# Loading the next stage's weights and first rows inside the stage in front of it, in a transformer kernel of eleven stages

## The chip, the cores and the metric

The kernel runs on one core of a Trainium2 chip. The metric is device time in microseconds (us) of one execution; lower is better. The core has five engines that each work through their own list of instructions: TensorE (PE; PEld is its weight load), VectorE (DVE), ScalarE (ACT), GpSimd (POOL) and SyncE (SP), which here mostly starts DMA transfers. Engines wait for one another, and for transfers, by semaphores.

## What is computed

Eight layers follow one another on x (32 sequences of 256 rows of 256 numbers), with a context of 32 x 120 x 192:

```python
x = x + _L0_xattn_ref(_layernorm(x, axis=-1), ctx_768, ...)    # 16 heads, Wq Wk Wv Wo
x = x + _L0_ffn_ref(_layernorm(x, axis=-1), L0_ffn_w1, L0_ffn_conv_w, L0_ffn_conv_b, L0_ffn_w2)
x = x + _L1_xattn_ref(_layernorm(x, axis=-1), ctx_768, ...)
x = x + _L1_ffn_ref(_layernorm(x, axis=-1), ...)               # 8 experts, top 2
x = x + _L2_xattn_ref(_layernorm(x, axis=-1), ctx_768, ...)    # 16 heads
x = x + _L2_ffn_ref(_layernorm(x, axis=-1), ...)               # 4 gated experts
x = x + _L3_xattn_ref(_layernorm(x, axis=-1), ctx_768, ...)    # sparse attention, FiLM, S4D, MLP
x = x + _L3_ffn_ref(_layernorm(x, axis=-1), ...)               # low rank
```

The three parts that the change touches:

```python
def weight_quant(w):                                   # L0 ffn: ternary weights
    scale = 1.0 / jnp.clip(jnp.mean(jnp.abs(w)), 1e-05)
    return jnp.clip(jnp.round(w * scale), -1, 1) / scale
...
hid = jax.nn.relu(jnp.einsum('td,edh->teh', xf, ew1) + eb1[None, :, :])   # L2 ffn: gated experts
y = jnp.einsum('teh,ehd->ted', hid, ew2) + eb2[None, :, :]
out = jnp.einsum('te,ted->td', dense_w, y)
...
scale_out, shift_out = jnp.split(c_t @ W_film_out + b_film_out, 2, axis=-1)   # L3 xattn, second half
y = y * (1.0 + mod_gate * scale_out) + mod_gate * shift_out
xt = x_text + y
h = layernorm(xt, g_ffn, b_ffn)
h = jax.nn.gelu(h @ W1 + b1, approximate=False) @ W2 + b2
return layernorm(xt + h, g_norm_out, b_norm_out)
```

## The kernel before

A stage works through the 32 sequences, one tile of 256 rows (two blocks of 128) at a time, as a pipeline written out in full: `pipeline` goes over slots, and in each slot an engine does its step of one tile and later steps of earlier tiles. The stages, by the first letters of their tiles in the profile: `a` (heads_attention, `a0`), then, overlapping in one block, `f` (ternary_feed_forward, `f0`), `a1`, a router, `v` and the experts `e`; then `a` again (heads_attention, `a2`), `fa` (adaptive_with_sparse_attention: the gated experts and the first half of L3's attention), `cv` (convolve_channels, the state-space part as Toeplitz matmuls), `m` (modulated_feed_forward, `m3`) and, overlapping with it, `f` (low rank, `f3`).

Between `a0` and `f0`, `a2` and `fa`, `fa` and `cv`, and `cv` and `m3` there is a boundary: SP waits until the stores have landed, clears the stage's semaphores one by one (`end_all`), and all engines pass a barrier. Only then does the next stage's program begin. SP takes its list in order, and all plain transfers are started by it; the only others are GpSimd's indirect gathers in `a2` and the experts.

What each of the three stages does first, before:

- `f0` (`start` of its `sync` and `vector`, L843 and L908): SP requests w1 (1 MB) into the one buffer `wf`, then the convolution's taps and bias. DVE sums |w1| (L912), PE adds up over partitions (L1071), DVE makes mean and reciprocal (L914, L917) and in three passes the ternary w1 (L920 to L924). SP waits for the last pass (`w_all`), requests w2 into the same `wf`, and only behind that the first rows `xb` (L853); DVE does the same five steps with w2, and a sum over w2 (L927). `wmean` and `wscale` count on the semaphore `consts`, on which POOL's 24 products for `diag` (L882) count too, so the reciprocal waits for these.
- `fa` (L2311 to L2330): SP requests eight small weights, then rows `xb` of tiles 0 and 1, then the experts' w1 and w2 (2 MB each) and the rest. DVE, ACT and PE wait for the eight small ones (`small`), DVE then for `xb` (L209). Rows of tile 2 can be requested once tile 0 is normalised (`xn_ready`). Per tile the gate's matmuls (L2785, L2793, L2794) lead to softmax steps on DVE (L2512 on) and ACT (L2688, L2690), and then come the experts' matmuls (L2808, L2820).
- `m3` (L3029, L3031): SP requests twelve weights, 3.5 MB; all engines wait for all of them (`weights`, 192), then PE multiplies Wv and W_film_out into one matrix (L3210).

In `a0` a tile also sends its row minimum out (L387, `a_lowest`) and back to all partitions (L395, `a_floor`, two transfers of 960 KB), which DVE needs at L539. In `a2` POOL gathers four pieces of 128 KB per tile (L430), which DVE combines (L493). In `cv` each of 16 groups of channels needs 2 MB, `cv_toep` (L2908), into one of two buffers.

## Time and profile before

| | us |
|---|---|
| median of 3 runs | 4808.49 (4806.17 to 4809.97) |
| the profiled execution's own time | 4787.28 |
| its span | 4785.5 |
| PE busy | 4430.9, 93% |
| DVE busy | 3206.7, 67% |
| ACT / POOL busy | 2044.3 / 2082.9, 43% / 44% |
| mean DMA rate | 85 GB/s |

The profile is of one execution, and its rows carry times from the span's start. PE is busy nearly all the time inside the stages; in forty equal slices its busy tenths fall to 5 in two (around 600 to 700 us and 2000 to 2100 us) and to 6 or 7 in a few others. A row of a timeline names the start, the duration, the engine (SPq is SP's starting of a transfer), the line, what is written and read, and in brackets how long the engine had been idle and what ended that.

### The profile page before, as it was taken

The numbers are of one execution on the slowest core, as the hardware profiler recorded it, in microseconds if no ns is written. First come the engines' busy times: TensorE is split into PE (matmuls) and PEld (weight loads), VectorE is DVE, ScalarE is ACT, GpSimd is POOL, SyncE is SP. The second block draws the span as 40 slices with busy tenths as digits, with TensorE's granted clock in tenths as the row PEclk, the third lists the DMA queues.
The fourth block names the chain that finished last, engine by engine and source line by source line (L and its number), as shares of the span: only waits on it lengthen the run. The fifth ranks groups of instructions, "written<-read, shape, count | busy, mean of one in ns | idle before, by whom it ended". The sixth has DMA issues, their size and how long they took to land. (4 is left out here: it accounts for less than half of the span.)

```text
span 4785.5 us, 90713 instructions
## 1 busy us (share of the span) xinstructions
PE 4430.9 (93%) x31788; PEld 3449.3 (72%) x31788; DVE 3206.7 (67%) x9688; ACT 2044.3 (43%) x4216; POOL 2082.9 (44%) x2505
## 2 busy tenths in 40 slices
PE   7999859999999999959999799999999877999999
PEld 5666547778875888846666688888888744777866
DVE  6888779997553333147776399999999943444444
ACT  3555447764443332224444244444444332222244
POOL 2222136553454233044443365655656503565532
PEclk9999979999999999979999899999999988999999
DMA  4666512236333222122221211111111083232233
GB/s 115 154 154 155 131 56 74 75 109 183 67 87 104 82 71 71 49 77 71 69 69 36 84 35 34 42 33 35 41 34 38 22 266 103 90 96 85 92 111 102
DMA packets 333274, 407.33 MB, mean 85 GB/s; under 512 B 58932, under 2 KB 294165, under 8 KB 322070
## 3 DMA queue, kind: packets, MB, share of 16 engines
q1 hardware_dynamic: 315190, 368.41, 27.1%
q0 software_dynamic: 13312, 25.25, 2.2%
q10 hardware_dynamic: 4320, 7.87, 0.6%
q8 instruction: 256, 4.19, 0.4%
q14 instruction: 196, 1.61, 0.1%
HBM read 304.45 MB, written 96.96 MB: 84 GB/s over the span
## 5 line engine op out<-in xcount | busy, mean ns | idle before, releaser
L2808 PE MATMUL fa_h<-fa_xnT,fa_w 128*128 128x256 f32 x2048 | 474.9, 383 | 0.0
L2820 PE MATMUL fa_y<-fa_w,fa_hT 128*128 128x256 f32 x2048 | 462.5, 379 | 0.0
L2820 PEld LDWEIGHTS fa_y<-fa_w,fa_hT 128*128 128x128 f32 x2048 | 386.5, 190 | 65.3 <-issue 15.4
L2808 PEld LDWEIGHTS fa_h<-fa_xnT,fa_w 128*128 128x128 f32 x2048 | 380.6, 191 | 56.5 <-issue 9.4
L2701 ACT ACTIVATE fa_hT<-fa_h,fa_b 128x256 f32<-128x256 f32 x512 | 215.0, 470 | 476.8 <-PE fa_h L2808 411.4
L516 DVE TENSOR_REDUCE a_mx<-a_score 128x16 f32<-128x1920 f32 x128 | 275.9, 2156 | 78.5 <-PE a_score L700 68.7
L1945 POOL DMA_INDIRECT e_xg<-moe_rows,e_idx x64 | 128.7, 2011 | 322.2 <-issue 244.8
L3187 ACT ACTIVATE m_hT<-m_h,m_b 128x256 f32<-128x256 f32 x256 | 107.5, 471 | 364.7 <-PE m_h L3250 364.7
L1695 PE MATMUL r_h<-r_xnT,r_rw 128*128 128x256 f32 x1024 | 248.2, 391 | 5.7 <-ACT r_hT L1646 5.7
L219 POOL TENSOR_SCALAR a_rs<-a_mv 128x2 f32<-128x2 f32 x96 | 21.4, 223 | 531.0 <-DVE a_mv L213 527.4
L2107 ACT ACTIVATE e_hT<-e_h,e_b 128x256 f32<-128x256 f32 x256 | 107.5, 471 | 329.5 <-PE e_h L2162 322.4
L3250 PE MATMUL m_h<-m_hnT,m_w 128*128 128x256 f32 x1024 | 235.7, 379 | 2.5 <-ACT m_hnT L3177 2.5
L3250 PEld LDWEIGHTS m_h<-m_hnT,m_w 128*128 128x128 f32 x1024 | 194.0, 190 | 53.8 <-issue 13.6
L2162 PE MATMUL e_h<-e_xT,e_w 128*128 128x256 f32 x1024 | 231.7, 380 | 0.9 <-DVE e_xT L1959 0.9
L2174 PE MATMUL e_y<-e_w,e_hT 128*128 128x256 f32 x1024 | 226.5, 379 | 0.0
L3260 PE MATMUL m_y<-m_w,m_hT 128*128 128x256 f32 x1024 | 226.4, 379 | 0.0
L1695 PEld LDWEIGHTS r_h<-r_xnT,r_rw 128*128 128x128 f32 x1024 | 188.7, 192 | 41.8 <-ACT r_hT L1646 17.3
L2174 PEld LDWEIGHTS e_y<-e_w,e_hT 128*128 128x128 f32 x1024 | 194.2, 190 | 26.4
L2162 PEld LDWEIGHTS e_h<-e_xT,e_w 128*128 128x128 f32 x1024 | 191.7, 190 | 25.8 <-DVE e_xT L1959 1.1
L3260 PEld LDWEIGHTS m_y<-m_w,m_hT 128*128 128x128 f32 x1024 | 192.1, 190 | 25.2 <-issue 0.4
L750 PE MATMUL a_av<-a_pT,a_vp 120*32 120x256 f32 x2048 | 182.1, 386 | 26.6 <-DVE a_qa L530 25.2
L2626 DVE MATCH_REPLACE8 fa_left<-fa_top,fa_left 128x120 f32<-128x120 f32 x768 | 195.3, 268 | 0.0
(453 smaller groups left out, 11055.1 us busy)
## 6 DMA issues: line engine op xcount, KB each, us to landing
a_floor<-a_lowest SPq DMA_DIRECT2D x64, 960.0 KB, 11.2
cv_toep<-kernels SPq DMA_DIRECT2D x16, 2048.0 KB, 9.6
x<-a_xo SPq DMA_DIRECT2D x96, 256.0 KB, 3.1
f_xb<-x SPq DMA_DIRECT2D x64, 256.0 KB, 3.6
f_xres<-x SPq DMA_DIRECT2D x64, 256.0 KB, 2.9
a_xb<-x SPq DMA_DIRECT2D x64, 256.0 KB, 3.2
e_w<-in_L_ffn_ew SPq DMA_DIRECT2D x16, 1024.0 KB, 4.8
a_cb<-in_ctx SPq DMA_DIRECT2D x96, 90.0 KB, 1.9
```

The costliest lines, as they stand in the source:

```text
L516: c.add(dve.tensor_reduce(m, s_in, AX.X, ALU.max))
L750: pe.matmul(av[g * 32:(g + 1) * 32, m * S:(m + 1) * S], vp[it.at][:, (m * G + g) * E + e, :], pT[m][:, g, h * S:(h + 1) * S], start=h == 0 ...
L1695: last = pe.matmul(h_ps[m % 2][:, c, :], rw1[:, k, f:f + P], xnT[it.p][:, k, :], start=k == 0, stop=k == KD - 1)
L1945: pool.indirect_dma_start(xg[p][:, t, :], None, xn_all[:, :], bass.IndirectOffsetOnAxis(ap=idx[p][:, t:t + 1], axis=0), bounds_check=B * S ...
L2162: last = pe.matmul(h_ps[m][:, c, :], w1[e][:, k, f:f + P], xT[it.p][:, k, :], start=k == 0, stop=k == KD - 1)
L2174: last = pe.matmul(y_ps[it.p][:, t * D:(t + 1) * D], hT[it.p][:, k, t * P:(t + 1) * P], w2[e][:, k, :], start=k == 0, stop=k == KH - 1)
L2626: c.add(dve.match_replace(left[t][:, h, :], top[t][:, rnd, h, :], rows[:, h, :], TAKEN))
L2701: act.activation(hT[e % 2][:, 2 * m + c, :], h_ps[j % 2][:, c, :], ACT.Relu, bias=b1[:, f:f + 1]).then_inc(h_ready, 1)
L2808: last = pe.matmul(h_ps[j % 2][:, c, :], w1[:, e, k, f:f + P], xnT[it.p][:, k, :], start=k == 0, stop=k == KD - 1)
L2820: last = pe.matmul(bank[:, t * D:(t + 1) * D], hT[e % 2][:, k, t * P:(t + 1) * P], w2[:, e, k, :], start=k == 0, stop=k == KE - 1)
L3250: last = pe.matmul(h_ps[m % 2][:, c, :], w1[:, k, f:f + P], hnT[it.p][:, k, :], start=k == 0, stop=k == KD - 1)
L3260: last = pe.matmul(y_ps[:, t, :], hT[it.p][:, k, t * P:(t + 1) * P], w2[:, k, :], start=k == 0, stop=k == KH - 1)
```

## The change

Three objects of a new class `Held` each own a piece of SBUF at its upper end: 16,640 bytes per partition for `f0` (`f0w`), 49,152 for `fa` (`faw`) and 31,488 for `m3` (`m3w`). They hold the stage's weights and, for `fa` and `m3`, the row buffers `xb`, with tiles 0 and 1 loaded in advance. The stage in front requests them: `a0` and `a2` in four parts behind the loads of their last four tiles (28 to 31), `cv` behind its last `cv_toep`, and at its end each waits for all of them. In `f0` w1 and w2 get a buffer each, and `wmean` and `wscale` count on a semaphore of their own.

```diff
@@ heads_attention
+                if it.i >= B - 4:
+                    held.load(sp, it.at, held_in)
...
             for p in two:
                 sp.wait_ge(stored[p], 16 * (B // 2))
+            sp.wait_ge(held_in, 16 * held.COUNT)
@@ TernaryHeld
+        super().__init__(nc, "f0w", 16640)
+        self.w, self.wf = w, [self.sb(f"wf{m}", [P, KD * H1]) for m in range(2)]
+        self.taps, self.cbias = self.sb("taps", [P, KH, 3]), self.sb("cbias", [P, KH])
+    def load(self, sp, part, done):
+        if part == 0:
+            sp.dma_start(self.wf[0][:], self.w["w1"].rearrange("p k n -> p (k n)")).then_inc(done, 16)
+        if part == 1:
+            sp.dma_start(self.wf[1][:], self.w["w2"].rearrange("p k n -> p (k n)")).then_inc(done, 16)
+        if part == 2:
+            sp.dma_start(self.taps[:], self.w["conv_w"]).then_inc(done, 16)
+            sp.dma_start(self.cbias[:], self.w["conv_b"]).then_inc(done, 16)
@@ ternary_feed_forward
-        def start():
-            sp.dma_start(wf[:], w["w1"].rearrange("p k n -> p (k n)")).then_inc(w_one, 16)
-            sp.dma_start(taps[:], w["conv_w"]).then_inc(weights, 16)
-            sp.dma_start(cbias[:], w["conv_b"]).then_inc(weights, 16)
-            sp.wait_ge(w_all, 4)
-            sp.dma_start(wf[:], w["w2"].rearrange("p k n -> p (k n)")).then_inc(w_one, 16)
...
-                dve.wait_ge(w_one, 16 * (m + 1))
-                dve.tensor_reduce(wsum[:, m:m + 1], wf[:], AX.X, ALU.add, apply_absolute_value=True).then_inc(sums, 1)
+                dve.tensor_reduce(wsum[:, m:m + 1], rows[:], AX.X, ALU.add, apply_absolute_value=True).then_inc(sums, 1)
                 dve.wait_ge(w_all, 4 * m + 1)
...
-                dve.wait_ge(consts, MADE + n)
+                dve.wait_ge(w_scale, 2 * m + 1)
@@ AdaptiveHeld.load (part 0: ew1; part 1: ew2; part 2: eight small ones)
+        if part == 3:
+            for a, n in ((self.wq, "Wq"), (self.wk, "Wk")):
+                sp.dma_start(a[:], v[n]).then_inc(done, 16)
...
+            for p in range(2):
+                sp.dma_start(self.xb[p][:], self.src[p]).then_inc(done, 16)
@@ adaptive_with_sparse_attention
             def load(it):
+                if opening(it):
+                    for p in two:
+                        sp.dma_start(aT[SK:SK + 1, p * P:(p + 1) * P], const["ones"][0:1, :]).then_inc(last_row, 16)
                 if it.reused():
                     sp.wait_ge(xn_ready, it.i - 1)
-                sp.dma_start(xb[it.p][:], src_v[it.i]).then_inc(x_in[it.p], 16)
+                    sp.dma_start(xb[it.p][:], src_v[it.i]).then_inc(x_in[it.p], 16)
...
-            dve.wait_ge(small, 128)
             dve.wait_ge(padded, 2)
@@ convolve_channels
                 sp.dma_start(toep[it.p][:], rows).then_inc(t_in[it.p], 16)
+                if it.i == D // CG - 1:
+                    held.load(sp, held_in)
 
             pipeline(sp, D // CG, 3, [(0, load)])
+            sp.wait_ge(held_in, 16 * held.COUNT)
@@ ModulatedHeld
+    def load(self, sp, done):
+        for p in range(2):
+            sp.dma_start(self.xb[p][:], self.src[p]).then_inc(done, 16)
+        for a, n in ((self.wf, "W_film_out"), (self.wv, "Wv"), (self.w1, "W1"), (self.w2, "W2"), (self.b1, "b1"), (self.gf, "g_ffn"), (self.bff, "b_ffn")):
+            sp.dma_start(a[:], self.w[n]).then_inc(done, 16)
+        for a, n in ((self.bf, "b_film_out"), (self.gate, "mod_gate"), (self.gout, "g_norm_out"), (self.bout, "b_norm_out"), (self.b2, "b2")):
+            sp.dma_start(a[:], self.w[n].partition_broadcast(P)).then_inc(done, 16)
@@ modulated_feed_forward
-            dve.wait_ge(weights, 192)
-            act.wait_ge(weights, 192)
-            pe.wait_ge(weights, 192)
```

How instructions stand now. SP at the boundary from `a0` to `f0`, before (`x<-a_xo` are the last stores; the ISA rows are the barrier and the clearing of semaphores):

```order
L383 DMA x<-a_xo 128x2x256 x3
L363 UNCONDITIONAL_BRANCH
L193 ISA x49
L111 UNCONDITIONAL_BRANCH
L844 DMA f_wf<-in_L_ffn_w 128x2048
L845 DMA f_taps<-in_L_ffn_conv_w 128x24
L846 DMA f_cbias<-in_L_ffn_conv_b 128x8
L848 DMA f_wf<-in_L_ffn_w 128x2048
L853 DMA f_xb_7048<-x 128x2x256
```

SP of the changed kernel at the tiles 28 and 29 of `a0`, where the two ternary weights now are:

```order
L401 DMA a_lowest<-a_low 8x2x256
L409 DMA a_floor<-a_lowest 120x2048 x2
L390 DMA a_xb<-in_x 128x2x256
L391 DMA a_cb<-in_ctx 96x240
L812 DMA f0w_wf_105<-in_L_ffn_w 128x2048
L397 DMA x<-a_xo 128x2x256
L401 DMA a_lowest<-a_low 8x2x256
L409 DMA a_floor<-a_lowest 120x2048 x2
L390 DMA a_xb<-in_x 128x2x256
L391 DMA a_cb<-in_ctx 96x240
L814 DMA f0w_wf_106<-in_L_ffn_w 128x2048
L397 DMA x<-a_xo 128x2x256
```

Each weight moved in front of the barrier, behind a tile's two `a_floor` and in front of its store; behind the barrier SP now has the first rows at once.

SP at the boundary from `cv` to `m3`, before, from the end of `cv`'s block on:

```order
L111 UNCONDITIONAL_BRANCH
L3029 DMA m_wf<-in_L_xattn_W_film_out 128x1024
L3029 DMA m_wv<-in_L_xattn_Wv 128x384
L3029 DMA m_w_51017<-in_L_xattn_W 128x2048
L3029 DMA m_w_51018<-in_L_xattn_W 128x2048
```

And in the changed kernel, the last transfers of `cv` (seven rows between are left out) and the start of `m3`:

```order
L2946 DMA cv_toep<-kernels 128x16x256 x16
L3050 DMA m3w_xb_49739<-x 128x2x256
L3050 DMA m3w_xb_49740<-x 128x2x256
...
L3054 DMA m3w_bout<-in_L_xattn_b_norm_out 128x256
L3054 DMA m3w_b_49738<-in_L_xattn_b 128x256
L2938 UNCONDITIONAL_BRANCH
L204 ISA x11
L111 UNCONDITIONAL_BRANCH
L3100 DMA m_cb_51051<-in_ctx 96x240
```

The fourteen transfers moved from behind the barrier to directly behind the sixteenth `cv_toep`, in front of the barrier.

## Rows read from the trace of the kernel before

**Rows 1.** The page's busy times, with shares of the span.
```profile
PE 4430.9 (93%) x31788; PEld 3449.3 (72%) x31788; DVE 3206.7 (67%) x9688; ACT 2044.3 (43%) x4216; POOL 2082.9 (44%) x2505
```

**Rows 2.** Waits of PE: us in total, times, longest us.
```profile
PE fa_t L2769 <- DVE fa_xn L227: 31.3, 7, 18.4
PE f_aux L1071 <- DVE f_wsum L912: 28.4, 2, 14.7
```

**Rows 3.** Timeline from `a0` to `f0`: start us, us, engine, line, operation.
```profile
608.24 0.35 SPq L844 DMA_DIRECT2D f_wf<-in_L_ffn_w  x1
...
613.12 2.29 DVE L912 TENSOR_REDUCE f_wsum<-f_wf 128x1 f32<-128x2048 f32 x1 [10.57 <-DMA f_wf<-in_L_ffn_w]
...
628.44 2.29 DVE L912 TENSOR_REDUCE f_wsum<-f_wf 128x1 f32<-128x2048 f32 x1 [4.83 <-DMA f_wf<-in_L_ffn_w]
...
635.64 3.58 DVE L927 TENSOR_REDUCE f_wf<-f_w2q 128x256 f32<-128x2048 bf16 x1
...
639.47 0.74 DVE L209 BATCH_NORM_STATS2 f_st<-f_xb 128x6 f32<-128x256 f32 x2
```

**Rows 4.** Timeline from `a2` to `fa`.
```profile
2652.94 0.16 POOL L2383 MEMSET fa_lg<- 128x16 f32 x2 [47.77 <-POOLq L194]
...
2661.45 0.75 DVE L209 BATCH_NORM_STATS2 fa_st<-fa_xb 128x6 f32<-128x256 f32 x2 [14.40 <-DMA fa_xb<-x]
...
2664.59 11.70 SPq L2319 DMA_DIRECT2D fa_xb<-x  x2
...
2671.32 0.57 PE L2794 MATMUL fa_g<-fa_dw,fa_dT 128*128 128x1 f32 x2
2674.12 0.75 DVE L209 BATCH_NORM_STATS2 fa_st<-fa_xb 128x6 f32<-128x256 f32 x2 [9.56 <-DMA fa_xb<-x]
...
2675.80 0.16 DVE L2512 TENSOR_TENSOR fa_lg<-fa_g,fa_gb 128x8 f32<-128x8 f32 x1
...
2681.28 3.30 PE L2808 MATMUL fa_h<-fa_xnT,fa_w 128*128 128x256 f32 x8
...
2685.67 7.15 PE L2808 MATMUL fa_h<-fa_xnT,fa_w 128*128 128x256 f32 x32
```

**Rows 5.** One of the page's DMA issues: KB each, median us to landing.
```profile
fa_xb<-x SPq DMA_DIRECT2D x32, 256.0 KB, 2.7
```

**Rows 6.** Timeline from `cv` to `m3`.
```profile
3955.65 2.81 PE L2972 MATMUL cv_y<-cv_toep,cv_xg_back 128*32 128x256 f32 x64 [2.17 <-DMA cv_toep<-kernels]
...
3959.16 1.88 ACT L2945 COPY xin<-cv_t 128x512 f32<-128x512 f32 x2
...
3962.28 0.35 SPq L3029 DMA_DIRECT2D m_wf<-in_L_xattn_W_film_out  x1
...
3967.54 0.46 SPq L3031 DMA_DIRECT2D m_b<-in_L_xattn_b  x1
...
3977.30 5.58 PE L3210 MATMUL m_f<-m_wf,m_wv 128*96 128x512 f32 x8 [17.48 <-DMA m_b<-in_L_xattn_b]
```

**Rows 7.** Windows of 1 us there: busy of PE, PEld, DVE, ACT, POOL; PEclk, DMA share, GB/s.
```profile
3953.00:3954.00 1.00, 0.48 (x4) 0.24 (x3) 0.00 (x0) 1.00 (x2) 0.00 (x0) 1.00 0.82 257
3954.00:3955.00 1.00, 0.00 (x0) 0.00 (x0) 0.00 (x0) 0.70 (x1) 0.00 (x0) 1.00 0.12 42
...
3966.00:3967.00 1.00, 0.00 (x0) 0.00 (x0) 0.00 (x0) 0.00 (x0) 0.00 (x0) 0.50 1.01 421
...
3973.00:3974.00 1.00, 0.00 (x0) 0.00 (x0) 0.00 (x0) 0.00 (x0) 0.00 (x0) 0.50 0.23 83
```

**Rows 8.** A window of tile 28 in `a0`, the same columns.
```profile
467.00:468.00 1.00, 0.43 (x3) 0.11 (x2) 0.80 (x2) 1.00 (x1) 0.00 (x0) 1.00 0.03 10
```

**Rows 9.** SP's next request of a tile's row minimum in `a0`, from the timeline.
```profile
469.30 0.61 SPq L387 DMA_DIRECT2D a_lowest<-a_low  x1
```

**Rows 10.** Tile 28 of `a2`: the last gather, and DVE's combining, from the timeline.
```profile
2492.07 1.00 POOL L430 DMA_INDIRECT a_g<-moe_out,a_at  x1 [0.30 <-issue]
...
2496.93 1.70 DVE L493 SCALAR_TENSOR_TENSOR a_xb<-a_g,a_wgt,a_xb 128x256 f32<-128x256 f32 x4
```

More of the change, by code:

```diff
@@ L147, in take, with __init__, sb @@
         raise ValueError(f"no room for {size} bytes in {self.spans}")
+class Held:
+    def __init__(self, nc, name, size):
+        self.low = SBUF_END - size
+        self.st = Stage(nc, name, area=Area((self.low, SBUF_END)))
+    def sb(self, *shape):
+        return self.st.sb(*shape)
 class Chain:
@@ L340, in heads_attention @@
         first, combined = st.sem("first"), st.sem("combined")
-    weights, made, masks = st.sem("weights"), st.sem("made"), st.sem("masks")
+    assert nc.sbuf_base <= held.low
+    weights, made, masks, held_in = st.sem("weights"), st.sem("made"), st.sem("masks"), st.sem("held_in")
     x_in, c_in = ([st.sem(f"{n}{p}") for p in four] for n in ("x_in", "c_in"))
@@ L822, in ternary_feed_forward @@
     st.banks.close()
-    weights, w_one, w_all, sums, consts = (st.sem(n) for n in ("weights", "w_one", "w_all", "sums", "consts"))
+    w_scale, w_all, sums, consts = (st.sem(n) for n in ("w_scale", "w_all", "sums", "consts"))
     r_in, stored = ([st.sem(f"{n}{p}") for p in two] for n in ("r_in", "stored"))
@@ L2273, in adaptive_with_sparse_attention @@
     GT = 256
-    small, large, attn, wready, padded = (st.sem(n) for n in ("small", "large", "attn", "wready", "padded"))
+    assert nc.sbuf_base <= held.low
+    wready, padded = st.sem("wready"), st.sem("padded")
     x_in, r_in, stored, c_in, v_in, m_in, t_in = ([st.sem(f"{n}{p}") for p in two] for n in (
@@ L2763, in _ @@
         def _(pe):
-            pe.wait_ge(small, 128)
             def turn(bank, rows):
@@ L2800, in step @@
                 def step(it):
-                    if j == 0 and opening(it):
-                        pe.wait_ge(large, 32)
                     if it.reused(1) or j >= 2:
@@ L2896, in convolve_channels @@
     t_in = [st.sem(f"t_in{p}") for p in two]
+    assert nc.sbuf_base <= held.low
+    held_in = st.sem("held_in")
     gathered, r_done, reversed_, y_done, y_copied, turned, y_out = (
```

181 lines of the change are left out of this document (95 added, 86 removed).

## The prediction, made before the changed kernel was run

> **What bounds the kernel now.** I read the busy times first. TensorE is busy for 93% of the span [rows 1], so inside the stages only work taken from it, or from DVE where DVE holds it up, would count; this change takes none. What it can take is idle time at the boundaries, where every engine stands still behind a barrier. So I read the list of PE's waits next: its longest single waits stand at the starts of `f0` and `fa` (14.7 us and 18.4 us [rows 2]) and at that of `m3` (17.48 us [rows 6]). Third, the timelines of these three places, to see what the first useful instruction waits for, and what comes late next. Last, windows of 1 us with the DMA rate, because a transfer that moves in front of a barrier still has to find room there.
>
> The sums are made against the profiled execution (4787.28 us, span 4785.5). The three timed runs have a median of 4808.49, 21.2 above it; I take the difference to stay and subtract the gain from the median.
>
> **From `a0` to `f0`.** Before, w1 is requested at 608.24, DVE begins at 613.12, and tile 0's statistics begin at 639.47 [rows 3]. After, both weights lie in SBUF when the barrier opens, so DVE begins at about 608.3 (a semaphore more to clear, a row of SP's more). Its work per weight is read from the second one, which had no wait inside: 628.44 to 635.64 is 7.20 us [rows 3]. I use that for both; the first took longer because its reciprocal also waited for POOL's products, which its own semaphore ends. The sum over w2 and its copy take 635.64 to 639.47, 3.83 us. So tile 0 begins at 608.3 + 2 x 7.20 + 3.83 = 626.5 instead of 639.47: **12.9 us**. What is late next? The rows of tile 0 are now requested right behind the barrier and land in some 3 us (2.7 for the same size [rows 5]), 15 us early; POOL's products (6 us) end long before PE needs them. All later steps of `f0` hang on tile 0, so the gain stays. Bounds: 12 (DVE slowed a little by POOL beside it) to 13.
>
> **From `a2` to `fa`.** The barrier opens at 2652.94; the first statistics begin at 2661.45, held by the rows behind eight small transfers, and the next at 2674.12, held 9.56 us by tile 2's rows, which queue behind 4 MB of experts' weights [rows 4]. After, the first begin at about 2653.2, 8.2 us earlier. Tile 2's rows are requested 3.14 us behind that (2664.59 - 2661.45), and land 2.7 us later [rows 5], at 2659.1. That is no longer last: the gate's matmuls of tile 0 end 10.44 us behind the first statistics (2671.32 + 0.57 - 2661.45), at 2663.6, and DVE's softmax step L2512 waits for them. From there to the first experts' matmul it was 2681.28 - 2675.80 = 5.5 us. So that matmul begins at 2663.6 + 5.5 = 2669.1 instead of 2681.28: **12.2 us**. From it on PE has work nearly without a gap, so this is what the stage gains. Bounds: 8.2, if tile 2's rows are as late relative to tile 0 as before; 13.8, if the first eight experts' matmuls (3.30 us, 0.41 each) run as fast as the 32 behind them (7.15 us, 0.22 each) [rows 4].
>
> **From `cv` to `m3`.** Here the cover is missing. PE's first matmul was at 3977.30, 15.0 us behind the barrier's end at 3962.28 [rows 6]. The fourteen transfers, 31,488 bytes on 128 partitions, 4.03 MB, now follow the last `cv_toep`. That one keeps the DMA engines busy until about 3954.1: their share is 0.82 in the window from 3953 and 0.12 in the next [rows 7], and PE takes it at 3955.65. `cv` has 5.4 us of work left there (ACT ends at 3961.04 [rows 6]). So the transfers aren't done when `cv` is, and SP, which now waits for them in front of the barrier, keeps the barrier shut. How long? The twelve weights took from 3962.28 to 3977.3, of which the first 0.8 us went by before bytes moved: 14.2 us. The two row tiles come on top, 0.52 MB at 421 GB/s [rows 7], 1.2 us. From 3954.1 that gives 3969.5; from the end of `cv`'s work to SP's first request behind the barrier it was 3962.28 - 3961.04 = 1.24 us, so PE begins at about 3970.8: **6.5 us** instead of 15. The context and head weights, still requested behind the barrier, take 3 us, while PE's first step takes 5.58. Below, the bound is 5 us, if the transfers take a little longer with `cv`'s other work. Above, it is 10.9: the 14.2 us were not all traffic. Large weights moved at 421 GB/s, but at 3973 the share was 0.23 [rows 7], while the small, spread ones followed one another. If requests made early close these gaps, 4.03 MB at 421 GB/s are 9.6 us, plus 1.5 for landing (3955.65 - 3954.1), ready at 3965.2, and PE at 3966.4. I take the long form, as nothing shows that the gaps came from late requests: the last was made at 3967.54, 5 us ahead of them.
>
> The Trainium skill (DMA: Bandwidth & Descriptors, Bandwidth) has the HBM side bind at about 358 GB/s; this trace has 421 over the whole window of 3966 [rows 7]. By the page the 4.03 MB would take an estimated 11.3 us and the last figure would fall from 10.9 to 9.2.
>
> **What the stages in front pay.** In `a0` each of tiles 28 and 29 gets 1 MB behind its `a_floor` pair. The DMA engines fall idle at 467 (share 0.03 [rows 8]), and the next request in the chain to `a_floor` comes at 469.30 [rows 9]; 1 MB at 421 GB/s is 2.5 us, so the queue is free at about 469.3, just in time. Were it moved at half that rate, `a_floor` would come some 2.5 us late, twice: cost 0 to 5, I take 0.3. In `a2` each of tiles 28 and 29 gets 2 MB (5 us), and 30 and 31 about 0.8 MB each, beside the gathers. The last gather is begun at 2492.07 and DVE combines from 2496.93 without a wait [rows 10], 3.9 us behind its issue; a landing takes about 2.7 [rows 5], so 1.2 us of room. The gathers' 0.5 MB shared evenly with the weights takes 1.2 us more, about the room. Cost 0 to 5 (four tiles), I take 0.5. SP's sixteen requests of 0.47 us in tiles 30 and 31 delay only a store, two tiles ahead of the reuse of its buffer.
>
> The Trainium skill (same page, Queues, rings and completion order) says that each DMA engine goes round between the queues that have work, packet by packet; that is the even sharing assumed here, and it speaks for a small cost and against none. Were GpSimd's queue served first, the 0.5 would be 0.
>
> **The sum:** 12.9 + 12.2 + 6.5 - 0.8 = 30.8 us, and 4808.5 - 30.8 = 4777.7.
>
> **Rivals.** (A) The held transfers of `m3` run dense: its gain is 10.9 instead of 6.5 and the total 35.2, 4773.3. For it: 421 GB/s in the large ones. Against it: the gaps with requests waiting. (B) The front pays: late `a_floor` (5) and late gathers (5), or `fa` keeps only its 8.2; a total of about 18 to 22, 4788. For it: rooms of about 0 and 1 us. Against: PE waits little in these stages, and only four tiles of each are touched. (C) The waits only change place: all three stages in front wait for what they requested as long as the next ones did. For `f0` and `fa` this would need transfers that last over 100 us, since the requests of tile 31 come that far ahead; for `m3` alone it costs the 6.5 and leaves 24.3, 4784. For no gain at all, 4808. (D) Slower: PE's clock. At the boundaries PE idles and its granted clock falls to 0.50 [rows 7]. If PE, starting with less behind it, stayed at 0.5 into `fa`'s matmuls, each of them would take 0.41 instead of 0.22 us [rows 4], about half a microsecond lost in each. The gain is spent from 62 us of dense matmuls at the low clock on, and 85 us make it slower by over 10: 4819. Against it: in the trace the clock is back within the first eight experts' matmuls, and the idle gets shorter, not longer.
>
> **The numbers.** Forecast, 24 to 34 us gained: 0.62. A: 0.18. B, and `m3`'s part of C: 0.13. C, nothing gained: 0.05. D: 0.02. The timed runs can tell about 0.2% (9.6 us) from no change. So faster 0.93, same 0.05, slower 0.02. The range leaves out C, D and the ends of A and B: below, 12.9 + 13.8 + 10.9 gained and 2 for the spread of the runs give 4769; above, B gives 4788.
>
> **What would show it.** Right: in `f0` the first statistics 18 us behind the barrier; in `fa` 0.3 us behind it, and the first experts' matmul 16 us; at the end of `cv` about 8 us in which only DMA works, the barrier open at 3970.7 less what was gained before. Tiles 28 to 31 of `a0` and `a2` as long as those ahead of them. Wrong: any wait of DVE for `a_floor` or `a_g` that was not there, `cv`'s last group later than 3955.65 (less the gain), the experts' matmuls at 0.41 us for more than ten, or a first matmul of `m3` within 5 us of `cv`'s last.

## The result, and the profile after

| | before | after |
|---|---|---|
| median, us | 4809.23 (4806.17 to 4811.34, 4 runs) | 4772.12 (4768.99 to 4777.19, 4 runs) |
| ratio | | 0.9928, 95% interval 0.9916 to 0.994 |
| the profiled execution's own time | 4787.28 | 4771.23 |
| its span | 4785.5 | 4769.5 |

The changed kernel is 37 us faster by the medians, where 30.8 were forecast, and inside the range of 4769 to 4788. The profiles give another number: 16 us. Before the reasons can be judged, this has to be cleared up: either half of the measured gain comes from a place that the change doesn't touch, or the two profiles can't simply be subtracted. I take the boundaries first, since they are what the prediction was about.

From `a0` to `f0`, the timeline after:

```profile
609.63 2.29 DVE L936 TENSOR_REDUCE f_wsum<-f0w_wf 128x1 f32<-128x2048 f32 x1 [5.78 <-PEq L205]
...
616.91 2.28 DVE L936 TENSOR_REDUCE f_wsum<-f0w_wf 128x1 f32<-128x2048 f32 x1
...
624.10 3.58 DVE L949 TENSOR_REDUCE f0w_wf<-f_w2q 128x256 f32<-128x2048 bf16 x1
...
627.93 0.75 DVE L220 BATCH_NORM_STATS2 f_st<-f_xb 128x6 f32<-128x256 f32 x2
```

DVE begins 0.03 us behind the barrier (SP's first request behind it is at 609.60) and goes through both weights without a wait: 7.28 us for the first (616.91 - 609.63), 7.19 for the second, 3.83 for the sum. The first statistics stand 18.3 us behind the barrier (627.93 - 609.60). Before it was 31.2 ([rows 3], 639.47 - 608.24): **12.9 us**.

From `a2` to `fa`:

```profile
2658.72 0.16 POOL L2428 MEMSET fa_lg<- 128x16 f32 x2 [44.18 <-POOLq L205]
...
2658.92 0.75 DVE L220 BATCH_NORM_STATS2 fa_st<-faw_xb 128x6 f32<-128x256 f32 x2 [6.13 <-POOL fa_lg L2428]
...
2662.06 4.96 SPq L2375 DMA_DIRECT2D faw_xb<-x  x2
...
2664.86 0.75 DVE L220 BATCH_NORM_STATS2 fa_st<-faw_xb 128x6 f32<-128x256 f32 x2 [2.83 <-DMA faw_xb<-x]
...
2669.27 0.17 DVE L2556 TENSOR_TENSOR fa_lg<-fa_g,faw_gb 128x8 f32<-128x8 f32 x1 [2.64 <-PE fa_g L2834]
...
2674.76 3.52 PE L2846 MATMUL fa_h<-fa_xnT,faw_w 128*128 128x256 f32 x8
```

The rows of tile 2 land 2.8 us behind their request (2664.86) and are no longer last; what is late is the softmax step behind the gate's matmuls, 10.35 us behind the first statistics (10.44 expected). The first experts' matmul is 16.0 us behind the barrier (2674.76 - 2658.72); it was 28.3 ([rows 4], 2681.28 - 2652.94): **12.3 us**.

From `cv` to `m3`:

```profile
3955.37 1.88 ACT L2986 COPY xin<-cv_t 128x512 f32<-128x512 f32 x2
...
3962.00 5.08 PE L3261 MATMUL m_f<-m3w_wf,m3w_wv 128*96 128x512 f32 x8 [5.99 <-PEq L205]
```

and in windows of 1 us (busy time of PE, PEld, DVE, ACT, POOL; PEclk, DMA share, GB/s):

```profile
3951.00:3952.00 1.00, 1.00 (x24) 0.73 (x20) 0.00 (x0) 0.00 (x0) 0.00 (x0) 0.62 1.11 426
3954.00:3955.00 1.00, 1.00 (x16) 0.61 (x8) 0.00 (x0) 0.29 (x1) 0.00 (x0) 0.68 1.07 434
3956.00:3957.00 1.00, 0.00 (x1) 0.00 (x0) 0.00 (x0) 1.00 (x2) 0.00 (x0) 1.00 0.94 288
...
3958.00:3959.00 1.00, 0.00 (x0) 0.00 (x0) 0.00 (x0) 0.00 (x0) 0.00 (x0) 0.53 0.62 212
3959.00:3960.00 1.00, 0.00 (x0) 0.00 (x0) 0.00 (x0) 0.00 (x0) 0.00 (x0) 0.50 0.33 110
3960.00:3961.00 1.00, 0.00 (x0) 0.00 (x0) 0.00 (x0) 0.00 (x0) 0.00 (x0) 0.50 0.02 8
```

ACT, the last at work in `cv`, ends at 3957.25 (3955.37 + 1.88). The held transfers move until about 3960, and `m3`'s first matmul begins at 3962.00, 4.8 us behind ACT. Before, it was 16.3 us (3977.30 - 3961.04 [rows 6]): **11.5 us**. The gap that the share had at 3972 to 3974 [rows 7] isn't there: it tapers from 0.94 to 0.33.

Three boundaries give 12.9 + 12.3 + 11.5 = 36.7, about what the medians show. So the profile of before is the one that has to be asked.

### The profile page after: what moved, and what is told of

Same layout as the page of the kernel before. It is cut to its first block and busy times, and to the rows that moved or that the text cites. A ratio compares the mean times of both kernels' runs of the same rounds, so it can differ in the third digit from the quotient of the medians.

```text
span 4769.5 us, 90704 instructions
## 1 busy us (share of the span) xinstructions
PE 4437.6 (93%) x31788; PEld 3454.4 (72%) x31788; DVE 3205.2 (67%) x9688; ACT 2043.9 (43%) x4216; POOL 2086.4 (44%) x2505
## 5 line engine op out<-in xcount | busy, mean ns | idle before, releaser
L2846 PE MATMUL fa_h<-fa_xnT,faw_w 128*128 128x256 f32 x2048 | 475.1, 383 | 0.0
L2858 PE MATMUL fa_y<-faw_w,fa_hT 128*128 128x256 f32 x2048 | 462.5, 379 | 0.0
L2858 PEld LDWEIGHTS fa_y<-faw_w,fa_hT 128*128 128x128 f32 x2048 | 386.5, 190 | 65.3 <-issue 15.4
L2846 PEld LDWEIGHTS fa_h<-fa_xnT,faw_w 128*128 128x128 f32 x2048 | 380.6, 191 | 56.5 <-issue 9.4
L2743 ACT ACTIVATE fa_hT<-fa_h,faw_b 128x256 f32<-128x256 f32 x512 | 215.0, 471 | 478.0 <-PE fa_h L2846 412.1
L3241 ACT ACTIVATE m_hT<-m_h,m3w_b 128x256 f32<-128x256 f32 x256 | 107.5, 471 | 366.5 <-PE m_h L3301 366.5
L3301 PE MATMUL m_h<-m_hnT,m3w_w 128*128 128x256 f32 x1024 | 237.5, 381 | 2.5 <-ACT m_hnT L3231 2.5
L3301 PEld LDWEIGHTS m_h<-m_hnT,m3w_w 128*128 128x128 f32 x1024 | 195.1, 191 | 54.2 <-issue 13.6
L3311 PE MATMUL m_y<-m3w_w,m_hT 128*128 128x256 f32 x1024 | 226.4, 379 | 0.0
L3311 PEld LDWEIGHTS m_y<-m3w_w,m_hT 128*128 128x128 f32 x1024 | 192.1, 190 | 25.2 <-issue 0.4
```

The costliest lines, as they stand in the source:

```text
L2743: act.activation(hT[e % 2][:, 2 * m + c, :], h_ps[j % 2][:, c, :], ACT.Relu, bias=b1[:, f:f + 1]).then_inc(h_ready, 1)
L2846: last = pe.matmul(h_ps[j % 2][:, c, :], w1[:, e, k, f:f + P], xnT[it.p][:, k, :], start=k == 0, stop=k == KD - 1)
L2858: last = pe.matmul(bank[:, t * D:(t + 1) * D], hT[e % 2][:, k, t * P:(t + 1) * P], w2[:, e, k, :], start=k == 0, stop=k == KE - 1)
L3301: last = pe.matmul(h_ps[m % 2][:, c, :], w1[:, k, f:f + P], hnT[it.p][:, k, :], start=k == 0, stop=k == KD - 1)
L3311: last = pe.matmul(y_ps[:, t, :], hT[it.p][:, k, t * P:(t + 1) * P], w2[:, k, :], start=k == 0, stop=k == KH - 1)
```

## Where the two profiles differ beside the boundaries

**The kernel before, once more, unchanged.**

> The kernel before, unchanged, once more. The timed medians of before and after differ by 37 us, the two profiled executions only by 16 (4787.28 and 4771.23). Theory 1: the first profile of before was a lucky execution in one stretch whose length changes from one execution to the next, the router and what overlaps with it, where after's profile loses about 12 us against it. Then a new profile of before has its own time near 4808, and the stretch from 1150 to 1560 us is 10 to 20 us longer than in the first. Rival: a profiled execution of this kernel is always some 20 us shorter than a timed one; then the new profile is near 4787 again, with every boundary at the same time as in the first. The ratio of the times is 1.000 in either case.

Measured: 1.0009 (interval 1.0 to 1.0018) for the same code, and a profile of 4805.85, not 4787.28. Here is PE's transposing at the router's start (`r_t`) and the experts' matmul `e_h`, in the first profile of before, the second, and that of after: duration in ns (least, median, greatest), first and last start in us:

```profile
L1677 PE MATMUL r_t<-c_ident,r_xn x128: 272/273/307, 1177.4 to 1483.2; 128*128 128x128 f32 x128
L2162 PE MATMUL e_h<-e_xT,e_w x1024: 379/379/483, 1564.2 to 2021.0; 128*128 128x256 f32 x171
```

```profile
L1677 PE MATMUL r_t<-c_ident,r_xn x128: 272/273/418, 1176.5 to 1497.5; 128*128 128x128 f32 x128
L2162 PE MATMUL e_h<-e_xT,e_w x1024: 379/379/483, 1581.8 to 2038.7; 128*128 128x256 f32 x171
```

```profile
L1698 PE MATMUL r_t<-c_ident,r_xn x128: 272/273/306, 1167.4 to 1485.8; 128*128 128x128 f32 x128
L2183 PE MATMUL e_h<-e_xT,e_w x1024: 379/379/483, 1568.6 to 2025.5; 128*128 128x256 f32 x171
```

The router took 305.8 us in the first profile of before (1483.2 - 1177.4), 321.0 in the second, 318.4 after. In the fourteen profiles of this study it is between 314.3 and 324.6 us, that first one excepted. So the first profile caught an execution in which the router ran 15 us faster than in the second, and what follows it 3 us; the other stretches of the two agree within 1.5 us (the table below). The 3 us are not unusual: that stretch takes 80.9 to 84.9 us in thirteen of the profiles, and 88.0 in one. PE's waits there go the same way: `r_h` waits for ACT's `r_hT` (us in total, times, longest us) in the first profile of before,

```profile
PE r_h L1695 <- ACT r_hT L1646: 5.7, 10, 1.0
```

and in the second:

```profile
PE r_h L1695 <- ACT r_hT L1646: 15.6, 23, 1.3
```

That is 9.9 of the 15.2 us. Why the same program meets these waits ten times in one execution and over twenty times in another isn't shown; it stays open.

With the two ordinary profiles, `before_again` and `after_again` (a second one of the changed kernel, below), the difference can be laid out by stretch. Each number is the distance between two first or last starts in the view of one tile:

| stretch | before, 1st | before, 2nd | after, 1st | after, 2nd |
|---|---|---|---|---|
| span's start to `a0`'s last `a_xo` | 601.9 | 600.4 | 603.2 | 602.7 |
| to `f0`'s first statistics | 37.6 | 37.7 | 24.7 | 24.8 |
| to the router's first `r_t` | 537.9 | 538.4 | 539.5 | 537.9 |
| first to last `r_t` | 305.8 | 321.0 | 318.4 | 320.5 |
| to the first `e_h` | 81.0 | 84.3 | 82.8 | 82.8 |
| to `a2`'s first gather | 499.3 | 500.0 | 499.7 | 499.7 |
| to `a2`'s last `a_xo` | 582.9 | 582.9 | 583.8 | 583.2 |
| to `fa`'s first experts' matmul | 34.9 | 35.0 | 22.7 | 22.7 |
| to its last one | 1113.0 | 1113.2 | 1114.8 | 1115.4 |
| to `cv`'s first `cv_r` | 59.5 | 59.4 | 59.4 | 59.4 |
| to its last `cv_t` | 105.7 | 105.6 | 106.7 | 107.2 |
| to `m3`'s first `m_h` | 53.5 | 53.7 | 39.6 | 41.3 |
| to the last `f_y` | 764.7 | 764.6 | 766.4 | 764.6 |

The second columns differ by 34.0 us: 12.9 + 12.3 + 12.4 won at the three boundaries, 6.4 given back inside `a0`, `a2`, `fa` and `cv` (2.3, 0.3, 2.2, 1.6), and 2.8 of small differences in the stretches between. That agrees with the timed runs. The columns of one kernel differ by up to 1.8 us in stretches other than the router's and the one behind it, so of the 6.4 only `a0`'s 2.3 and `fa`'s 2.2 are more than that. Over all profiles `fa` took 1111.9 to 1113.2 us where its weights are loaded behind the barrier (four) and 1113.3 to 1115.4 where they are held (ten); `cv` took 103.5 to 107.3 with nothing held for `m3` and 104.1 to 107.6 with it, which overlap. The part of `a0` that could pay, from the `a_xo` written near 440 us (ahead of the first held request, at 474.90) to the last one, took 159.7 to 162.7 us in the five profiles whose `a0` loads nothing and 162.2 to 164.1 in the nine whose `a0` does, which overlap too. So only `fa`'s loss is clear of the spread, by 0.1 us.

## One part undone at a time

```diff
@@ no_f0: the function ternary_feed_forward is that of before
-        heads_attention(nc, const, "a0", ..., 10000.0, ternary)
+        heads_attention(nc, const, "a0", ..., 10000.0, None)
@@ no_fa: adaptive_with_sparse_attention is that of before
-        heads_attention(nc, const, "a2", ..., adaptive, routed)
+        heads_attention(nc, const, "a2", ..., None, routed)
@@ no_m3: modulated_feed_forward and convolve_channels are those of before
```

> The changed kernel with the first part undone: the ternary weights are again loaded behind the barrier, one after the other into one buffer, and a0 loads nothing for f0. The other two parts stay. If the parts add up in the timed runs and this one is worth what the traces show (first statistics 12.9 us earlier relative to the barrier), it is 12 to 13 us slower than the changed kernel, about 4785 (ratio to the kernel before 0.995). Rival: the gain of f0 is spent in the router stretch behind it, where after's trace loses about 12.6 us; then undoing it costs nothing, about 4772 (0.992).

> The changed kernel with the second part undone: fa's weights and first rows are again requested behind the barrier, and a2 loads nothing for fa. If the parts add up, it is 11 to 12 us slower than the changed kernel (12.2 at the start, less 0.5 to 1.5 that a2 pays), about 4783 (ratio 0.9946). Rival: held loads beside the gathers of a2 cost more than that, as a2 ended 0.9 us later relative to its start; then at most 10 us.

> The changed kernel with the third part undone: m3's twelve weights and two row tiles are again requested behind the barrier. My forecast gave this part 6.5 us, rival A 10.9. The trace of after has PE's first matmul of m3 15.3 - 3.8 = 11.5 us earlier relative to cv's last work. If that is the gain, this kernel is 11 to 13 us slower than the changed one, 4783 to 4785 (ratio 0.9949). If only the forecast's 6.5 is a gain of the whole, 4779 (0.9936). The three undone parts together should be 37 if they add up.

Measured against the kernel before: 0.9956 (0.9943 to 0.997), 0.9948 (0.9935 to 0.9962) and 0.9951 (0.9937 to 0.9964). The changed kernel has 0.9928 in its own series and 0.9935 in another; against the mean of these, 0.9931, the parts are worth 0.0025, 0.0017 and 0.0020, that is 12, 8 and 10 us of 4800, each uncertain by about 8, since both ratios have an interval. Their sum is 30 where the whole gives 31 to 35, so they add up as far as this can tell. The rival that the gain of `f0` is spent in the router forecast 0.992 for `no_f0`, which lies outside its interval, and falls. The rival for `fa`, at most 10 us because `a2` pays, isn't excluded: 8 us were measured, and `a2` took 581.1 us in `no_fa`, 2.1 to 2.7 less than in the two profiles of the changed kernel, though `a2` also varies from 579.7 to 586.0 over the ten profiles that load for `fa`. In the traces each undone boundary is back at its old length while the other two keep theirs within 1.8 us: last `a_xo` to first `f_st` 38.1 us in `no_f0` (24.7 after), last `a_xo` to first experts' matmul 35.0 in `no_fa` (22.7), last `cv_t` to first `m_f` 18.1 in `no_m3` (6.3).

## What is needed of `f0`'s part

```diff
         def start():
+            for part in range(3):
+                held.load(sp, part, w_in[min(part, 2)])
@@ vector
+                dve.wait_ge(w_in[m], 16)
                 dve.tensor_reduce(wsum[:, m:m + 1], rows[:], AX.X, ...)
```

> The changed kernel, but a0 loads nothing for f0: w1, w2, taps and bias are requested behind the barrier, each into its own held buffer, then the first rows. DVE waits for each weight. It splits the 12.9 us of f0 into prefetch and second buffer. By the steps of the prediction only the landing of w1 comes back (613.12 - 608.24 = 4.9 us); w2 lands while DVE works on w1 (7.2 us), so its wait of 4.8 us and the reciprocal's wait for POOL stay away. First statistics 23 us behind the barrier (31.2 before, 18.3 after), 5 us slower than the changed kernel and 8 us faster than with the part undone: ratio about 0.9939. Rival: the prefetch carries it all, 12 to 13 us slower than the changed kernel, 0.9955.

```profile
608.81 0.35 SPq L813 DMA_DIRECT2D f0w_wf<-in_L_ffn_w  x1
...
613.60 2.29 DVE L944 TENSOR_REDUCE f_wsum<-f0w_wf 128x1 f32<-128x2048 f32 x1 [10.55 <-DMA f0w_wf<-in_L_ffn_w]
...
620.68 2.28 DVE L944 TENSOR_REDUCE f_wsum<-f0w_wf 128x1 f32<-128x2048 f32 x1
...
631.89 0.74 DVE L220 BATCH_NORM_STATS2 f_st<-f_xb 128x6 f32<-128x256 f32 x2
```

In this timeline DVE waits for the first weight only (613.60 - 608.81 = 4.8 us) and not for the second; the first statistics come 23.1 us behind the barrier, as expected to 0.1. So 8 of the 12.9 us are due to the second buffer and the separate semaphore (which of the two gives how much was not tried), and 4.8 to loading in front of the barrier. The timed runs give 0.9949 (0.9936 to 0.9963) beside 0.9935 of the changed kernel in the same series, 7 us, uncertain by 6: they agree, but alone wouldn't tell 5 from 12.

## Why `m3`'s held transfers ran dense

**The small ones first, behind the barrier** (on the kernel before):

```diff
-            for a, n in ((wf, "W_film_out"), (wv, "Wv"), (w1, "W1"), (w2, "W2"), (b1, "b1"), (gf, "g_ffn"), (bff, "b_ffn")):
+            for a, n in ((b1, "b1"), (gf, "g_ffn"), (bff, "b_ffn")):
                 ...
             for a, n in ((bf, "b_film_out"), (gate, "mod_gate"), (gout, "g_norm_out"), ...):
                 ...
+            for a, n in ((wf, "W_film_out"), (wv, "Wv"), (w1, "W1"), (w2, "W2")):
+                ...
```

> The kernel before with one edit: m3 requests its eight small and broadcast weights first and the four large ones last, all behind the barrier as before. It asks why the held transfers of m3 ran dense where I expected them to keep their gaps. Theory 1, the order: the gap at 3971 to 3975 of the kernel before (share down to 0.15) is the start-up of small, spread transfers with no large one left to cover them. With the large ones last it is covered; 3.53 MB at 421 GB/s are 8.4 us, so PE's first matmul comes 11 to 12 us behind SP's first request instead of 15.0, and the kernel is 3 to 4 us faster than the one before (ratio 0.9993, near what can be measured; the trace decides). Theory 2: the small ones cost the same 4 to 5 us wherever they stand, or slow the others; then 15 us again and 1.000.

Measured: 1.0013 (1.0004 to 1.0023), not faster. Its timeline and windows:

```profile
3984.11 0.35 SPq L3029 DMA_DIRECT2D m_b<-in_L_xattn_b  x1
...
4000.74 3.73 PE L3212 MATMUL m_f<-m_wf,m_wv 128*96 128x512 f32 x4 [19.09 <-DMA m_w<-in_L_xattn_W]
```

```profile
3988.00:3989.00 1.00, 0.00 (x0) 0.00 (x0) 0.00 (x0) 0.00 (x0) 0.00 (x0) 0.50 0.16 32
...
3995.00:3996.00 1.00, 0.00 (x0) 0.00 (x0) 0.00 (x0) 0.00 (x0) 0.00 (x0) 0.50 1.03 434
```

PE begins 16.6 us behind the first request, not 11 to 12, and not 15.0. Theory 1 falls: large transfers requested behind the broadcast ones don't fill their gaps (share 0.16 to 0.42 from 3988 to 3992, with large ones requested from 3987.82 on). The view of DMA issues shows how slowly these five run (KB, median us from issue to landing):

```profile
m_bf<-in_L_xattn_b_film_out SPq DMA_DIRECT2D x1, 256.0 KB, 3.4
...
m_gout<-in_L_xattn_g_norm_out SPq DMA_DIRECT2D x1, 128.0 KB, 4.7
m_bout<-in_L_xattn_b_norm_out SPq DMA_DIRECT2D x1, 128.0 KB, 5.5
m_b<-in_L_xattn_b SPq DMA_DIRECT2D x1, 128.0 KB, 6.4
...
m_gate<-in_L_xattn_mod_gate SPq DMA_DIRECT2D x1, 0.5 KB, 4.1
```

They are issued 0.47 us apart but land 1.1 to 1.4 us apart, 0.5 KB as slowly as 128 KB.

**The same order, held, behind `cv`'s last transfer** (on the changed kernel):

> The changed kernel with m3's held transfers in the other order, still behind cv's last cv_toep: the eight small and broadcast ones first, then the four large ones, then the rows. Behind the barrier that order made it slower: first matmul 16.6 us behind the first request instead of 15.0, the broadcast ones landing some 1.2 us apart with nothing beside them. Theory 1, cover: what takes time in the broadcast ones is their start-up, which the cv_toep in flight hides when they are requested early; then the order costs nothing here and m3's first matmul stands 4 to 6 us behind cv's last work on ACT, as in the changed kernel (4.8). Theory 2, order: they take their 5 us of the queue wherever they stand, if nothing large is in front of them in m3's own list; then 6.5 to 8 us.

This is one execution, so only its timeline and windows are read:

```profile
3952.84 1.88 ACT L2986 COPY xin<-cv_t 128x512 f32<-128x512 f32 x2
...
3962.54 1.99 PE L3263 MATMUL m_f<-m3w_wf,m3w_wv 128*96 128x512 f32 x2 [9.04 <-PEq L205]
```

```profile
3947.00:3948.00 1.00, 0.35 (x7) 0.19 (x11) 0.00 (x0) 0.00 (x0) 0.00 (x0) 0.90 0.29 93
3949.00:3950.00 1.00, 1.00 (x20) 0.58 (x15) 0.00 (x0) 0.00 (x0) 0.00 (x0) 0.50 0.27 96
3952.00:3953.00 1.00, 0.88 (x13) 0.57 (x6) 0.00 (x0) 0.74 (x2) 0.00 (x0) 1.00 1.03 419
```

`m3`'s first matmul stands 7.8 us behind ACT's end (3962.54 - 3954.72), inside the 6.5 to 8 of theory 2. The gap is back, from 3946 to 3951, although the broadcast ones were requested at 3942.55 to 3945.61, while the last `cv_toep` moved. So it isn't enough that something large is in flight. The changed kernel has both: large ones of the same list ahead of the broadcast ones, and `cv_toep` ahead of these; each of the other three lists lacks one or both. It is also the only list with nothing requested behind its broadcast ones (in the kernel before, rows, context and head weights follow, 0.7 MB; in the other two the large ones), and no run tells these apart. Its broadcast ones landed 9.3 to 9.5 us behind their requests, within 3 us of one another; in the kernel before it was 6.7 to 9.7, with 2.7 MB ahead of them. Counted from the end of the dense part, they took about 6.6 us before (3970.6 to 3977.2), 5.3 in `held_small_first` and 4 after. That the five cost some 2 to 3 us less in the changed kernel's list than in that of before is measured; which of the differences does it is not.

## Versions that go further

**`m3`'s weights in `fa`**, where the DMA engines idle:

```diff
@@ adaptive_with_sparse_attention, load
+                if it.i >= B - 4:
+                    later.early(sp, it.i - (B - 4), held_in)
@@ ModulatedHeld: behind the last cv_toep only
+        for p in range(2):
+            sp.dma_start(self.xb[p][:], self.src[p]).then_inc(done, 16)
```

> The changed kernel with m3's twelve weights requested in fa, three to five of them behind the rows of each of its last four tiles, into free SBUF below fa's own weights; only the two row tiles (0.5 MB) are left behind the last cv_toep. fa has nearly idle DMA engines. In the changed kernel m3's first matmul is 4.8 us behind cv's last work on ACT, and cv's last 64 matmuls take 4.43 us at a lower clock where they took 2.81. With the 3.5 MB gone, the barrier should open about 1.3 us behind ACT: 3 to 5 us faster than the changed kernel, ratio 0.992. Rival: fa's tail pays for it (its last tiles' stores, films and masks queue behind 1 MB each, 2.5 us) and nothing is left: 0.9928, as the changed kernel.

```profile
3952.48 1.88 ACT L2991 COPY xin<-cv_t 128x512 f32<-128x512 f32 x2
...
3955.71 5.04 PE L3276 MATMUL m_f<-m3w_wf,m3w_wv 128*96 128x512 f32 x8 [2.57 <-PEq L206]
```

`m_f` begins 1.35 us behind ACT's end, as expected, and 6.3 us earlier than after (6.9 than in `after_again`). Of this 3.5 us are won at the boundary (last `cv_t` to first `m_f` 2.8 us, 6.3 in both profiles of the changed kernel); the rest stands in stretches ahead of it that vary by as much. `fa` is as long as in the changed kernel (1115.1). The timed runs show 0.993 (0.9916 to 0.9943) beside 0.9935 in the same series: 3 us, less than they can tell. The comparison kernel in that series:

> The changed kernel once more, in the same series as the others, so that they can be compared with it directly. Ratio 0.9928 (0.992 to 0.994). In its trace the boundaries should stand as in the first (first statistics of f0 18.3 us behind its barrier, first experts' matmul of fa 16 us, m3's first matmul 4.8 us behind cv's last work), while the stretch of the router (first to last r_t of PE), which was 305.8 us in the first trace of before and 314 to 321 in the five others, is free to change by 10 us. If it does, the spread of the timed runs comes from there.

Measured: 0.9935 (0.9921 to 0.9948); its trace is the last column of the table above, with the three boundaries at 24.8, 22.7 and 41.3 us. The router took 320.5 us, so between the two profiles of the changed kernel it moved by 2.1 us only.

**And `cv`'s first transfer in `fa`:**

```diff
-    toep = [st.sb(f"toep{p}", [P, CG, S]) for p in two]
+    toep = [held.toep, st.sb("toep1", [P, CG, S])]
@@ load
+                if it.i == 0:
+                    return
```

> The kernel m3_in_fa with one exchange: fa's last tiles also load cv's first cv_toep (2 MB), and in its place m3's two largest weights (W1 and W2, 2 MB) go back behind cv's last cv_toep, with the two row tiles. cv then needs 15 transfers of 2 MB behind its barrier, not 16. In the changed kernel cv moves 340 GB/s from 3850 to 3940 with its DMA engines busy throughout, and PE waits 12.3 us in all for cv_toep. If the transfers bound cv, it gets 5 to 6 us shorter (from cv's first cv_r to its last cv_t, 106.7 in the changed kernel, about 101). The 2.5 MB at the end take 6 us, about what cv's work behind its last transfer takes (7 us), so the barrier opens as early as in m3_in_fa. Against the changed kernel 9 to 12 us by the traces, ratio to the kernel before 0.991. Rival: PE's own work (2.81 + 1.98 + 1.43 = 6.2 us a group, 99.5 us in all) is as long as the transfers, and cv stays at 105; then no more than 2 us better than m3_in_fa.

`cv` took 104.1 us, not 101 (and 107.2 in `toep_and_stores` below, which has the same edit). That is the rival's number, but its reason, that PE's own work takes as long as the transfers, isn't what the trace shows. PE still waits for them, first in the changed kernel, then in this one (us in total, times, longest us):

```profile
PE cv_y L3013 <- DMA cv_toep<-kernels: 12.3, 16, 2.5
```

```profile
PE cv_y L3021 <- DMA m3w_toep<-kernels: 6.8, 7, 1.7
PE cv_y L3021 <- DMA cv_toep<-kernels: 4.8, 7, 3.0
```

That is 11.6 us instead of 12.3. What was saved at the start went into a gap: there are two buffers, so the third transfer can be requested only when PE has used the first one, and PE begins with that at 3861.85, when DVE has prepared its other operand. The second transfer is through at about 3862, and the DMA engines stand idle until the third moves:

```profile
3862.00:3864.00 2.00, 2.00 (x52) 1.44 (x49) 1.68 (x2) 0.58 (x1) 0.00 (x0) 1.00 0.00 0
```

```profile
3861.85 2.81 PE L3021 MATMUL cv_y<-m3w_toep,cv_xg_back 128*32 128x256 f32 x64
...
3864.79 0.39 SPq L2953 DMA_DIRECT2D m3w_toep<-kernels  x1
```

In the changed kernel the first two transfers run one behind the other through this time. Once the gap is over, the DMA engines are as full as there: share 1.06 and 340 GB/s from 3866.7 to 3936.7, 1.06 and 337 in the same part of the changed kernel's `cv` (3860 to 3930). So from the third transfer on, the transfers still set the pace of `cv`. Whether a third buffer would bring the missing 3 us was not tried. Timed: 0.9914 (0.9901 to 0.9928), the lowest so far, though its interval overlaps that of the changed kernel.

**The early store.** The stage boundary from the experts to `a2` had the same shape as those that the change removes: SP waits for stores, and one of them is started last though its data have long been there.

```diff
@@ experts, store
+            if it.i == N - 3:
+                sp.wait_ge(made, 2)
+                sp.dma_start(kpad[:, 0:LP]..., zero[:]).then_inc(k_stored, 16)
+                sp.wait_ge(k_left, GROUPS + 1)
+                sp.dma_start(kpad[:, LP:LP + S]..., kout[:]).then_inc(k_stored, 16)
```

> The kernel toep_in_fa with a second edit in the experts: the two stores of the state-space kernels (e_zero and e_kout to kernels) are started behind the store of the third last tile instead of at the very end. In the changed kernel e_kout is complete at 1949 but its store is issued at 2041.44 and takes 7.2 us to land, and the barrier to a2 waits for it (a2's first request at 2057.34), while the last store of the experts themselves, issued at 2040.4, lands some 3 us later. If that store is what ends last, a2 starts 5 to 6 us earlier against the experts' last e_h (first gather 2068.3 - 2025.5 = 42.8 us behind it, then about 37), and the whole is 14 to 18 us faster than the changed kernel, ratio 0.990. Rival: the 4096 small packets of that store beside the experts' last transfers delay a weight or a gather by as much, or another wait ends as late; then as toep_in_fa.

```profile
2040.11 0.32 SPq L1935 DMA_DIRECT2D moe_out<-e_yo  x1
2050.89 0.34 SPq L380 DMA_DIRECT2D a_wq<-in_L_xattn_Wq  x1
```

From the last `e_h` to `a2`'s first gather it is 36.0 us (42.8 after, 42.2 in `toep_in_fa`, 40.7 to 43.1 in all thirteen other profiles), 6 to 7 less than in these two, as expected. From the experts' last store to `a2`'s first request it is 10.8 us (2050.89 - 2040.11), where it was 16.9 in the changed kernel (2057.34 - 2040.40). Timed: 0.9911 (0.9898 to 0.9925), median 4766.19, the fastest of all but not to be told from `toep_in_fa` (0.9914), and 3 us less than it where 6 were expected. Against the changed kernel's 0.9928 and 0.9935 the intervals touch; the traces of their boundaries, not the ratios, are what speaks for it. PE's longest single wait in the kernel before is at this boundary, behind `a2`'s first requests, and the prediction's list of the longest waits left it out (the columns are total, times, longest):

```profile
PE a_front L646 <- DVE a_bvw L474: 38.0, 2, 24.9
```

**All held requests behind the last tile:**

```diff
-                if it.i >= B - 4:
-                    held.load(sp, it.at, held_in)
+                if it.i == B - 1:
+                    for part in range(4):
+                        held.load(sp, part, held_in)
```

> The changed kernel, but a0 and a2 request all that they hold for the next stage behind tile 31 alone instead of in four parts behind tiles 28 to 31: 2.1 MB at once in a0, 5.6 MB (some 13 us at 421 GB/s) at once in a2. It asks what room the front stages had, where I took 0.3 and 0.5 us. If the wait views are right that these stages hardly wait for DMA at their end, both end as in the changed kernel (a2 from its first gather to its last a_xo 583.8 and 583.2 us there, 581 to 583 where it loads nothing) and the ratio is the changed kernel's, 0.993. Rival: a burst holds up a gather or an a_floor, by up to 13 us in a2 and 5 in a0; then up to 0.997, and a wait of DVE for a_g or a_floor shows in tiles 30 or 31.

In `a2` the burst fills the DMA engines (shares 0.89 and 0.98) (windows of 5 us):

```profile
2550.00:2555.00 5.00, 4.46 (x75) 2.64 (x70) 2.96 (x3) 0.25 (x1) 2.75 (x3) 1.00 0.89 232
2555.00:2560.00 5.00, 5.00 (x55) 3.90 (x51) 4.12 (x8) 3.76 (x6) 0.00 (x0) 1.00 0.98 396
```

and DVE waits for no gather. Its only wait for a transfer from there on, or in `a0` from 440 us on, is this one in `a0`:

```profile
DVE a_pT L555 <- DMA a_floor<-a_lowest: 0.7, 1, 0.7
```

`a0` and `a2` took 605.0 and 585.4 us, 2 us more each than in `after_again`; of `a0`'s 2.3 us, 1.3 are there at 440 us, before the first held request. The ratio is 0.9944 (0.993 to 0.9957), next to 0.9935 for the changed kernel in another series. So one burst costs no visible wait of DVE, and at most a few microseconds; the rival's 0.997 lies outside the interval.

## Why the prediction was right, and where it was off

- **Median against profile.** "I take the difference to stay" is the step that decided whether 4777.7 or something 20 us lower stood there. It was the right choice, but for a reason that I did not have: 18.5 of the 21 us were one fast passage of the router and the stretch behind it in the profiled execution, not a fixed distance. That it came out right owes something to luck. The changed kernel's profile has no such passage, and its time is within 1 us of its median. Whoever had forecast the profile's own time from the profile (4787.3 - 30.8 = 4756.5) would have missed it by 15 us.
- **`a0` to `f0`, 12.9.** Measured 12.9, and by the steps given: 7.28 and 7.19 us for a weight, 3.83 for the sum. The first scaling pass, beside POOL's products, took 1.48 us, the second 1.28, which is the slowing that the lower bound allowed for.
- **`a2` to `fa`, 12.2.** Measured 12.3, with each step of it: request 3.14 us behind the first statistics, landing 2.8 us later, softmax step at 10.35 us, first experts' matmul 5.5 us on.
- **`cv` to `m3`, 6.5.** This is the mis-sized term: 11.5 measured up to the first `m_f`, and 12 to 14 up to the first `m_h` (from the first `m_f` to the first `m_h` it takes 31.8 us in `no_m3`, 33.3 after and 35.7 before, so the first number is the cleaner one). The failed step is "I take the long form, as nothing shows that the gaps came from late requests". Rival A's 10.9 was the better number. Where it put the first matmul 5.4 us behind ACT's end (3966.4 - 3961.04), it stood 4.8 behind it. My own sign for being wrong, "a first matmul of `m3` within 5 us of `cv`'s last", was met if it's counted from ACT's end (4.8 us), and not from `cv`'s last matmul (6.0). Two things are in the 5.0 us. Counted from PE's taking of the last `cv_toep` to the first `m_f`, it was 21.7 us before (3977.30 - 3955.65) and 11.8 after (3962.00 - 3950.23): 9.9 us gained, so 3.4 of the error are transfers that ended earlier than I took. The other 1.6 are `cv`'s own last work, which took that much longer after and so covered more; they are paid again in `cv`, as the next point says. The mechanism (SP keeps the barrier shut until the transfers have landed) was right: `m3_in_fa` takes this rest away, and its `m_f` begins 1.35 us behind ACT.
- **The cost in front, 0.8.** Sized too small as a whole. `a0` and `a2` pay 2.3 and 0.3 us in the table, no more than profiles of one kind differ; the 1.6 of `cv` and the 2.2 of `fa` were not in the sum at all. In `cv` the place is seen: its last 64 matmuls, behind an idle time of 2.49 us, took 4.43 us with PEclk at 0.5 to 0.68 where they took 2.81 [rows 6]. The slower end (4.12 to 4.49 us) is in seven of the ten profiles whose `cv` loads something for `m3` and in none of the four whose `cv` loads nothing; but in `no_fa` and `toep_in_fa` the same 64 took 2.81 us beside held transfers and behind idle times of 2.47 and 2.97 us. So it isn't shown that the held transfers cause it. For `fa` no place was found.
- **Rivals.** B (late `a_floor`, late gathers) fell with `late_all`: even a burst of 5.6 MB holds up no gather. C fell: no stage in front but `cv` waits for what it holds. D fell: the clock is back as early as before (3.52 us for the first eight experts' matmuls, 7.15 for the 32 behind them, as in [rows 4]).

In total, 30.8 + 5.9 (`m3`'s term, up to the first `m_h`: 12.4 instead of 6.5) + 0.1 (`fa`) - 5.6 (the front, 6.4 instead of 0.8) + 2.8 (the stretches between) = 34.0 us in the traces, and 31 to 37 in two series of timed runs. The two large errors, 5.9 too little and 5.6 too much, nearly cancel, and that is luck.

The Trainium skill (DMA: Bandwidth & Descriptors, Bandwidth) has the HBM side bind at about 358 GB/s. The held weights again moved faster: 426 and 434 GB/s in two windows shown above; `cv_toep`, in rows of 1 KB, moved about 340. The same section has 425 GB/s measured for 16 MB with the neighbouring core idle; the two windows agree with that, and not with 358.

## What to carry to other kernels

At the two boundaries whose stage in front had idle DMA engines, the forecast gain of work that no longer waits behind the barrier was met to 0.1 us, though the stages together gave back some 6 us elsewhere; but look for the cheap half first, since here a second buffer and a semaphore of its own gave 8 of 12.9 us without any prefetch. A transfer requested at the very end of a stage kept the barrier shut here, be it a load or a store, and also where its data were ready long before: read what SP waits for last. And before two profiles are subtracted, take a second one of the same kernel; here one stage ran 15 us faster in one execution than in the next.
